# Expert stage of a mixture-of-experts layer: tiles of 256 tokens, stationary weights in the first product, biases as columns

## The chip, the core and the metric

The kernel runs on one core of one Trainium2 chip. The metric is the device time of one execution in microseconds (us). The core has five engines that run apart from each other and meet at semaphores: PE (TensorE, matrix products), DVE (VectorE), ACT (ScalarE), POOL (GpSimd) and SP (which here only issues transfers).

## The reference, cut to what matters

There are two layers in sequence. The first normalises the tokens, modulates them, and sends every token to 2 of 8 experts; the second is a transformer layer that the change leaves alone. Of the first layer the expert part is

```python
N = h_flat.shape[0]                                     # 16 * 256 = 4096 tokens, D = 256, E = 8, FF = 1024
hid = jax.nn.relu(jnp.einsum('nd,edf->nef', h_flat, exp_w1) + exp_b1)
eout = jnp.einsum('nef,efd->ned', hid, exp_w2) + exp_b2
y = jnp.einsum('ned,ne->nd', eout, combine)             # combine: two gates per token, else 0
return x + y.reshape(x.shape)
```

The kernel computes only the two experts that a token chose: 8192 pairs of token and expert.

## The kernel before

The function `condition_and_route` has three stages: conditioning, routing over 16 blocks of 256 tokens (`pipeline`), and the expert stage. `transformer` follows and reads the experts' rows back by gather.

**Expert stage.** Routing writes the token rows of each expert into a region of its own in memory (`dispatch`), and each region is cut into tiles of `P` = 128 tokens. Since the counts are known only at run time, the loop always runs over the largest number of tiles that can occur, `TILES` = (8192 - 128) / 128 + 8 = 71; a small table (`tile_tab`) gives the expert and the first row of each. All expert weights lie on chip in float32 (`w1`, `w2`).

Each product is made of three passes over operands that are split into an upper part (rounded to fp32r, `hi`) and the rest (`lo`): hi·hi, hi·lo, lo·hi (`PASSES`). So for every tile the weights of its expert are split again, 4 pieces of 128x512 for each product: ACT rounds (`upper_w1` L406, `upper_w2` L412), then DVE subtracts for the first product (`lower_w1` L714) and POOL for the second (L351).

One tile t goes this way:

- SP loads the rows (`load`) and both biases, repeated over 128 partitions (`load_b1` 512 KB, `load_b2`).
- PE turns the rows (`turn_in` L478, 2 transposes); ACT and DVE split them (`take_in` L394, `lower_tokens` L719).
- `up` (L489): 12 products, the turned tokens stationary, 512 columns of weights moving; the result has tokens on the partitions. DVE adds the bias (`take_hidden` L709).
- PE turns the 1024 hidden features (`turn_hidden` L497, 8 transposes); ACT takes the relu and rounds (`relu` L400), DVE makes the rest (`lower_hidden` L700).
- `down` (L507): 24 products of 256 columns; DVE adds the bias (`take_out` L727), SP stores.

The order on every engine is that of the code: each engine runs `tile_loop` with a `body` of its own, and an engine that waits holds everything behind it. The stage is a pipeline over two tiles: in one turn of the loop PE runs the first product of tile t and the second of tile t - 1,

```python
            if a_tile(t - 1):
                turn_hidden(t - 1)
            if a_tile(t):
                up(t)
            if a_tile(t + 1):
                turn_in(tile.ahead(1))
            if a_tile(t - 1):
                down(t - 1)
```

and DVE finishes the hidden features of tile t - 1 first, then splits `w1` for tile t + 1, two pieces before and two after the second half of `take_hidden`.

Of the kernel before, what the change touches and what calls it, by code (L numbers as in the profile page):

```python
# [7 lines left out]
F32 = mybir.dt.float32  # L8
# [8 lines left out]
P = 128  # L17
# [8 lines left out]
REGION = B * T + P  # L26
TILES = (K * B * T - P) // P + E
# [83 lines left out]
def condition_and_route(nc, ctx, io, keep):  # L111
# [78 lines left out]
    htok = [xin[0][:, i, :] for i in range(2)]  # L190
    y = xin[1][:, 0, :]
    hid = token_rows[:].rearrange("p i n -> p (i n)")
# [6 lines left out]
    b1 = [sb(f"b1_row{i}", [P, FF]) for i in range(2)]  # L199
# [17 lines left out]
    cond = cond_weights(nc, sb, ada_w, sty_w2)  # L217
# [12 lines left out]
    def _(sp):  # L230
# [1535 lines left out]
```

## Time and profile before

| | us |
|---|---|
| median of 3 runs | 1499.03 (1496.92 to 1502.69) |
| the profiled execution, its own time | 1499.17 |
| its span in the trace | 1497.0 |
| PE busy / DVE busy / ACT busy / POOL busy | 1295.6 / 1138.4 / 963.0 / 738.3 |

The span is the time from the first to the last event of the trace; some 2 us of the execution's time lie outside it. A busy PE is not a PE at its peak, since its products overlap: of two that follow each other closely, the distance between their starts is the cost, not the duration printed. "PEclk" and the column after POOL in a table of stretches are the TensorE clock that was granted, as a share of full speed (1.0 is 2.4 GHz, 0.5 is 1.2 GHz). The expert stage lies between about 165 and 689 us.

### The profile page before, as it was taken

To read this page: it belongs to the slowest core of one execution; us is meant where nothing else is said; L and a number is where in the kernel's file an instruction comes from. 1 tells how busy PE (TensorE), PEld (TensorE's weight loads), DVE (VectorE), ACT (ScalarE), POOL (GpSimd) and SP (SyncE) were. 2 spreads that over 40 slices of the span, in tenths; PEclk is the share of its full clock that TensorE was granted. 3 is DMA by queue.
4 is the path that set the end of the run, shared out by engine and by line. 5 is a ranking of instruction groups with operands and counts; after the bars stand their busy time and mean duration, and the time that the engine had idled before them with its cause. 6 is when DMAs were issued, how large, how long until landed. Compare 5 with 4: busy or idle time off the path is not lost. (4 is left out here: it accounts for less than half of the span.)

```text
span 1497.0 us, 36973 instructions
## 1 busy us (share of the span) xinstructions
PE 1295.6 (87%) x9225; PEld 1126.6 (75%) x9225; DVE 1138.4 (76%) x3159; ACT 963.0 (64%) x2326; POOL 738.3 (49%) x645
## 2 busy tenths in 40 slices
PE   2666499999999999994579999999999999999996
PEld 2555388888888888883468878888788877788875
DVE  3888799999999999995657666676666775666652
ACT  2222388888888888881166666666666666676671
POOL 1677488888888888884212323223232332322211
PEclk9999999999999999996799999999999999999997
DMA  3676333333433434344666665566655566555520
GB/s 115 210 239 221 125 133 127 126 126 126 134 127 125 128 124 135 127 127 141 202 222 191 215 190 184 168 189 211 196 182 172 185 210 204 175 184 167 184 78 14
DMA packets 197678, 241.07 MB, mean 161 GB/s; under 512 B 20720, under 2 KB 176560, under 8 KB 197616
## 3 DMA queue, kind: packets, MB, share of 16 engines
q1 hardware_dynamic: 184816, 202.70, 42.9%
q10 hardware_dynamic: 6624, 20.84, 4.3%
q0 software_dynamic: 6176, 16.79, 3.2%
q8 instruction: 28, 0.46, 0.1%
q14 instruction: 34, 0.28, 0.1%
HBM read 196.36 MB, written 39.71 MB: 158 GB/s over the span
## 5 line engine op out<-in xcount | busy, mean ns | idle before, releaser
L351 POOL TENSOR_TENSOR w_lo<-w,w_hi 128x512 fp32r<-128x512 f32 x284 | 422.7, 1518 | 100.2 <-ACT w_hi L412 100.2
L1176 ACT ACTIVATE bias<-bias,neg_max 128x256 f32<-128x256 f32 x512 | 255.3, 501 | 200.8 <-DVE neg_max L1488 200.3
L714 DVE TENSOR_TENSOR w_lo<-w,w_hi 128x512 fp32r<-128x512 f32 x284 | 302.0, 1102 | 1.0 <-ACT w_hi L406 1.0
L412 ACT ACTIVATE w_hi<-w 128x512 fp32r x284 | 179.2, 632 | 54.0 <-PE ps_y L507 35.8
L1488 DVE CUSTOM_DVE_ANT_0 bias<-ps_s,bias 128x256 f32<-128x256 f32 x512 | 194.2, 416 | 20.2 <-PE ps_s L1264 13.1
L406 ACT ACTIVATE w_hi<-w 128x512 fp32r x284 | 173.3, 632 | 21.7 <-DVE tile_tab L683 11.0
L1128 POOL TENSOR_TENSOR act_lo<-up_f,act_hi 128x512 fp32r<-128x512 f32 x64 | 82.5, 1289 | 209.3 <-ACT act_hi L1220 209.3
L507 PE MATMUL ps_y<-w_hi,hidT_hi 128*128 128x256 f32 x568 | 168.8, 297 | 14.8 <-DVE hidT_lo L700 14.2
L1262 PE MATMUL ps_s<-mask_f,minus_ident 128*128 128x256 f32 x512 | 155.4, 325 | 28.4 <-DVE neg_max L1488 15.9
L1276 PE MATMUL ps_p<-const,bias 128*128 128x128 f32 x1024 | 157.5, 277 | 13.7 <-ACT bias L1176 13.6
L507 PE MATMUL ps_y<-w_hi,hidT_lo 128*128 128x256 f32 x568 | 161.7, 285 | 0.0
L507 PE MATMUL ps_y<-w_lo,hidT_hi 128*128 128x256 f32 x568 | 161.3, 284 | 0.0
L1110 POOL TENSOR_TENSOR rstd<-mv,minus_half 128x2 f32<-128x2 f32 x32 | 23.1, 722 | 258.9 <-DVE mv L1547 171.9
L1262 PEld LDWEIGHTS ps_s<-mask_f,minus_ident 128*128 128x128 f32 x512 | 99.7, 195 | 60.9 <-DVE neg_max L1488 34.4
L1264 PE MATMUL ps_s<-k_stack,q_stack 128*128 128x256 f32 x512 | 135.2, 285 | 0.0
L1276 PEld LDWEIGHTS ps_p<-const,bias 128*128 128x128 f32 x1024 | 117.1, 141 | 22.4 <-issue 12.4
L507 PEld LDWEIGHTS ps_y<-w_hi,hidT_hi 128*128 128x128 f32 x568 | 109.2, 192 | 32.0 <-DVE hidT_lo L700 23.7
L489 PE MATMUL ps_h<-w_hi,htokT_hi 128*128 128x512 f32 x284 | 118.2, 416 | 0.9 <-DVE htokT_lo L719 0.9
L1182 ACT ACTIVATE probT<-ps_p 128x512 f32<-128x512 f32 x176 | 102.3, 581 | 24.7 <-PE ps_p L1276 24.7
L489 PE MATMUL ps_h<-w_hi,htokT_lo 128*128 128x512 f32 x284 | 112.8, 397 | 0.0
L489 PE MATMUL ps_h<-w_lo,htokT_hi 128*128 128x512 f32 x284 | 111.9, 394 | 0.0
L507 PEld LDWEIGHTS ps_y<-w_lo,hidT_hi 128*128 128x128 f32 x568 | 109.4, 193 | 0.0
(266 smaller groups left out, 3330.3 us busy)
## 6 DMA issues: line engine op xcount, KB each, us to landing
bias<-bias_dram SPq DMA_DIRECT2D x128, 512.0 KB, 3.8
b_row<-b_dram SPq DMA_DIRECT2D x71, 512.0 KB, 3.6
w<-w_dram ACTq DMA_DIRECT2D x32, 512.0 KB, 4.7
xin<-dispatch SPq DMA_DIRECT2D x71, 128.0 KB, 2.2
b_row<-b_dram SPq DMA_DIRECT2D x71, 128.0 KB, 3.1
expert_out<-xin SPq DMA_DIRECT2D x71, 128.0 KB, 1.7
q_stack<-q_hi_rows SPq DMA_DIRECT2D x64, 128.0 KB, 2.9
k_stack<-k_hi_rows SPq DMA_DIRECT2D x64, 128.0 KB, 2.9
```

The costliest lines, as they stand in the source:

```text
L351: pool.tensor_tensor(w2_part["lo"][:, k, :], w2_piece(e, k), w2_part["hi"][:, k, :].bitcast(F32), ALU.subtract).then_inc(sem("w2_split"), 1)
L406: act.activation(w1_part["hi"][:, k, :], w1_piece(e, k), ACT.Copy).then_inc(sem("w1_upper"), 1)
L412: act.activation(w2_part["hi"][:, k, :], w2_piece(e, k), ACT.Copy).then_inc(sem("w2_upper"), 1)
L489: last = pe.matmul(ps_h[i][:, :], htokT[a][:, c, :], w1_part[b][:, k, :], start=(c == 0 and n == 0), stop=(c == C - 1 and n == 2))
L507: last = pe.matmul(ps_y[:, 0:D], hidT[a][:, f * P:(f + 1) * P], w2_part[b][:, k, (f % 2) * D:(f % 2 + 1) * D], start=(f == 0 and n == 0), ...
L714: dve.tensor_tensor(w1_part["lo"][:, k, :], w1_piece(e, k), w1_part["hi"][:, k, :].bitcast(F32), ALU.subtract).then_inc(sem("w1_split"), 1)
L1176: act.activation(head_rows(h, j), head_rows(h, j), ACT.Exp, scale=-1.0, bias=neg_max[par][:, h, j:j + 1], accum_out=total[par][:, h, j:j + ...
L1182: act.activation(probT[:, h % (2 * GROUP), :, :], halves(ps_p[h % 2][:, :]), ACT.Copy).then_inc(sem("pT_scalar"), 1)
L1262: pe.matmul(ps_s[h % 2][:, j * T:(j + 1) * T], minus_ident[:], mask_f[par][:, j, :], start=True, stop=False)
L1264: last = pe.matmul(ps_s[h % 2][:, j * T:(j + 1) * T], q_stack[par][:, h, j * P:(j + 1) * P].bitcast(F32R), k_stack[par][:, h // 2, :].bitc ...
L1276: last = pe.transpose(ps_p[h % 2][:, kt * T + j * P:kt * T + (j + 1) * P], head_rows(h, j)[:, kt * P:(kt + 1) * P], ident)
L1488: dve.tensor_tensor_reduce(head_rows(h, j), ps_s[h % 2][:, j * T:(j + 1) * T], head_rows(h, j), -1.0, LARGEST, ALU.add, ALU.min, neg_max[p ...
```

## The change

The tile grows to `TOK` = 256 tokens, so `TILES` is (8192 - 256) / 256 + 8 = 39. In `up` the weights become the stationary operand and the 256 turned tokens the moving one: 48 products of 256 columns for a tile, and the result comes out with the features on the partitions, so that `turn_hidden` goes away. The bias is then one number per partition: `b1` is loaded once as columns, ACT adds it within the relu (one instruction for each of 8 feature blocks) and writes float32 to a ring of four slots, `hid`. DVE rounds pairs of blocks (`split_hidden`), and DVE (pairs 0 and 2) and POOL (pairs 1 and 3) make the rest (`lower_pair`). `down` has 48 products into two banks. The work on a tile is no longer spread over two turns of the loop: `up(t)`, `turn_in(t + 1)` and `down(t)` stand behind each other. Small weights of the conditioning move into the room of the last expert's `w1`, and ACT waits for their use before it loads that.

```diff
-REGION = B * T + P
-TILES = (K * B * T - P) // P + E
+TOK = 256
+REGION = B * T + TOK
+TILES = (K * B * T - TOK) // TOK + E
...
-
-    htokT = {n: sb(f"htokT_{n}", [P, C, P], F32R) for n in ("hi", "lo")}
-    hidT = {n: sb(f"hidT_{n}", [P, FF], F32R) for n in ("hi", "lo")}
+    htok = [buf[:] for buf in xin]
+    y = h2
+    hid = columns[:].rearrange("p i n -> p (i n)").rearrange("p (s m) -> p s m", s=HID_SLOTS)
+
+    htokT = {n: sb(f"htokT_{n}", [P, C, TOK], F32R) for n in ("hi", "lo")}
+    hidT = {n: sb(f"hidT_{n}", [P, F, TOK], F32R) for n in ("hi", "lo")}
...
-    b1 = [sb(f"b1_row{i}", [P, FF]) for i in range(2)]
+    b1 = sb("b1_columns", [P, E, F])
...
+    ps_t = bank("ps_t")
+    ps_h = [bank(f"ps_h{i}") for i in range(F // 2)]
+    ps_y = [bank(f"ps_y{j}") for j in range(J)]
+    ps_h0, ps_h1, ps_logit, ps_rank = ps_h
+    ps_back = ps_y[0]
...
+    def lower_pair(eng, t, g):
+
+        rows = slice(2 * g, 2 * g + 2)
+        slots = slice(2 * g % HID_SLOTS, 2 * g % HID_SLOTS + 2)
+        return eng.tensor_tensor(hidT["lo"][:, rows, :], hid[:, slots, :], hidT["hi"][:, rows, :].bitcast(F32), ALU.subtract)
...
+        sp.dma_start(b1[:], io["b1"]).then_inc(sem("b1_in"), 16)
...
-        def load_b1(tile):
-            wait_free(sp, sem("hid_ready"), 2 * (tile.t - 1), alone=True)
-            row = io["b1"][bass.ds(expert_of(tile.t), 1), :].rearrange("e n -> (e n)")
-            sp.dma_start(b1[tile.par][:], row.partition_broadcast(P)).then_inc(sem(f"b1_in{tile.par}"), 16)
...
+        def lower_hidden(t, g):
+            wait_alone(pool, sem("hid_rounded"), 2 * t + g // 2 + 1)
+            lower_pair(pool, t, g).then_inc(sem("hidT_odd"), 1)
+
+        def lower_w2(t, e, k):
+            wait_alone(pool, sem("w2_upper"), PARTS * t + k + 1)
+            pool.tensor_tensor(w2_part["lo"][:, k, :], w2_piece(e, k), w2_part["hi"][:, k, :].bitcast(F32),
+                               ALU.subtract).then_inc(sem("w2_split"), 1)
+
         def body(tile):
...
+            t = tile.t
+            if a_tile(t):
+                e = pool.value_load(tile_tab[0:1, 0, bass.ds(t, 1)], min_val=0, max_val=E - 1)
+                lower_hidden(t, 1)
+                lower_w2(t, e, 0)
+                lower_w2(t, e, 1)
+                lower_hidden(t, 3)
+                lower_w2(t, e, 2)
+                lower_w2(t, e, 3)
...
+            wait_free(act, sem("up_done"), F * t)
+            act.activation(htokT["hi"][:], ps_t[:, :].rearrange("p (c m) -> p c m", c=C), ACT.Copy).then_inc(sem("htokT_upper"), 1)
+
+        def relu(t, e, f):
+            if f % 2 == 0:
+                g = f // 2
+                wait_alone(act, sem("up_done"), F * t + f + 2)
+                wait_free(act, sem("hidT_odd" if g % 2 else "hidT_even"), 2 * t + g // 2, alone=True)
+            act.activation(hid[:, f % HID_SLOTS, :], ps_h[f // 2][:, (f % 2) * TOK:(f % 2 + 1) * TOK], ACT.Relu,
+                           bias=b1[:, bass.ds(e, 1), f:f + 1].rearrange("p e f -> p (e f)")).then_inc(sem("hid_ready"), 1)
+
+        def upper_w1(t, e, k):
+            wait_free(act, sem("up_done"), F * (t - 1) + 4 * (k // C + 1), alone=True)
+            act.activation(w1_part["hi"][:, k, :], w1_piece(e, k), ACT.Copy).then_inc(sem("w1_upper"), 1)
+
+        def upper_w2(t, e, k):
+            wait_free(act, sem("w2_used"), PARTS * (t - 1) + k + 1, alone=True)
+            act.activation(w2_part["hi"][:, k, :], w2_piece(e, k), ACT.Copy).then_inc(sem("w2_upper"), 1)
+
+        def expert_of(t):
+            return act.value_load(tile_tab[0:1, 0, bass.ds(t, 1)], min_val=0, max_val=E - 1)
 
         def body(tile):
             t = tile.t
-            if a_tile(t - 1):
-                relu(t - 1)
+            if a_tile(t):
+                e = expert_of(t)
+                for f in range(4):
+                    relu(t, e, f)
             if a_tile(t + 1):
-                upper_w1(t + 1)
+                ahead = expert_of(t + 1)
+                for k in range(PARTS):
+                    upper_w1(t + 1, ahead, k)
                 take_in(t + 1)
             if a_tile(t):
-                upper_w2(t)
-
+                for f, pieces in ((4, ()), (5, (0,)), (6, (1,)), (7, (2, 3))):
+                    relu(t, e, f)
+                    for k in pieces:
+                        upper_w2(t, e, k)
...
+                for j in range(J):
+                    last = pe.transpose(ps_t[:, c * TOK + j * P:c * TOK + (j + 1) * P], htok[tile.par][:, j, c * P:(c + 1) * P], ident)
             last.then_inc(sem("tile_turned"), 1)
 
         def up(t):
             pe.wait_ge(sem("htokT_split"), t + 1)
...
-
-        def turn_hidden(t):
-            pe.wait_ge(sem("hid_ready"), 2 * (t + 1))
-            wait_free(pe, sem("hidT_split"), 2 * t)
             for f in range(F):
-                last = pe.transpose(ps_th[f // 4][:, (f % 4) * P:(f % 4 + 1) * P], hid[:, f * P:(f + 1) * P], ident)
-            last.then_inc(sem("hid_turned"), 1)
+                if f % 4 == 0:
+                    pe.wait_ge(sem("w1_split"), PARTS * t + C * (f // 4 + 1))
+                if f % 2 == 0:
+                    wait_free(pe, sem("hid_ready"), F * (t - 1) + f + 2)
+                for c in range(C):
+                    for n, (a, b) in enumerate(PASSES):
+                        last = pe.matmul(ps_h[f // 2][:, (f % 2) * TOK:(f % 2 + 1) * TOK],
+                                         w1_part[a][:, C * (f // 4) + c, (f % 4) * P:(f % 4 + 1) * P], htokT[b][:, c, :],
+                                         start=(c == 0 and n == 0), stop=(c == C - 1 and n == 2))
+                last.then_inc(sem("up_done"), 1)
 
         def down(t):
-            pe.wait_ge(sem("hidT_split"), 2 * (t + 1))
             wait_free(pe, sem("y_ready"), t)
             for k in range(PARTS):
                 pe.wait_ge(sem("w2_split"), PARTS * t + k + 1)
+                pe.wait_ge(sem("hidT_odd" if k % 2 else "hidT_even"), 2 * t + k // 2 + 1)
                 for f in (2 * k, 2 * k + 1):
...
+                    for j in range(J):
+                        for n, (a, b) in enumerate(PASSES):
+                            last = pe.matmul(ps_y[j][:, 0:D], hidT[a][:, f, j * P:(j + 1) * P],
+                                             w2_part[b][:, k, (f % 2) * D:(f % 2 + 1) * D],
+                                             start=(f == 0 and n == 0), stop=(f == F - 1 and n == 2))
...
         def body(tile):
             t = tile.t
-            if a_tile(t - 1):
-                turn_hidden(t - 1)
             if a_tile(t):
                 up(t)
             if a_tile(t + 1):
...
+        def split_hidden(t, g):
+            dve.wait_ge(sem("hid_ready"), F * t + 2 * (g + 1))
+            wait_free(dve, sem("w2_used"), PARTS * (t - 1) + g + 1)
+            rows = slice(2 * g, 2 * g + 2)
+            slots = slice(2 * g % HID_SLOTS, 2 * g % HID_SLOTS + 2)
+            rounded = dve.tensor_copy(hidT["hi"][:, rows, :], hid[:, slots, :])
+            if g % 2:
+                rounded.then_inc(sem("hid_rounded"), 1)
+            else:
+                rounded.then_inc(sem("hid_upper"), 1)
+                dve.wait_ge(sem("hid_upper"), 2 * t + g // 2 + 1)
+                lower_pair(dve, t, g).then_inc(sem("hidT_even"), 1)
...
-            dve.tensor_tensor(y, ps_y[:, 0:D], b2[tile.par][:], ALU.add).then_inc(sem("y_ready"), 1)
+            wait_free(dve, sem(f"y_sent{tile.par}"), 16 * tile.before)
+            for j in range(J):
+                last = dve.tensor_tensor(y[tile.par][:, j, :], ps_y[j][:, 0:D], b2[tile.par][:], ALU.add)
+            last.then_inc(sem("y_ready"), 1)
 
         def body(tile):
             t = tile.t
             if a_tile(t + 1):
                 e = dve.value_load(tile_tab[0:1, 0, bass.ds(t + 1, 1)], min_val=0, max_val=E - 1)
-            if a_tile(t - 1):
-                lower_hidden(t - 1)
+                for k in range(PARTS):
+                    lower_w1(t + 1, e, k)
+                lower_tokens(t + 1)
             if a_tile(t):
-                take_hidden(tile, 0)
-            if a_tile(t + 1):
-                lower_w1(t + 1, e, 0)
-                lower_w1(t + 1, e, 1)
-            if a_tile(t):
-                take_hidden(tile, 1)
-            if a_tile(t + 1):
-                lower_tokens(t + 1)
-                lower_w1(t + 1, e, 2)
-                lower_w1(t + 1, e, 3)
+                for g in range(F // 2):
+                    split_hidden(t, g)
             if a_tile(t - 1):
                 take_out(tile.ahead(-1))
```

How the order on DVE changes: the rows below are what DVE runs in one turn of `tile_loop` (a straight copy of it ahead of the loop). `columns` is the room of `hid` after the change, `token_rows` that of `hid` before and of `y` after. Before:

```order
L700 SCALAR_TENSOR_TENSOR hidT_lo<-ps_th,hidT_hi 128x512 [waits hidT_upper] x2
L709 TENSOR_TENSOR token_rows<-ps_h,b_row 128x512 [waits hid_turned,b1_in1,w1_used]
L714 ISA [waits w1_upper]
L714 TENSOR_TENSOR w_lo<-w,w_hi 128x512
...
L709 TENSOR_TENSOR token_rows<-ps_h,b_row 128x512 [waits w1_used]
L719 TENSOR_TENSOR htokT_lo<-ps_t,htokT_hi 128x256 [waits htokT_upper]
...
L727 TENSOR_TENSOR xin<-ps_y,b_row 128x256 [waits b2_in0,w2_used]
```

And after, the last piece of `w1` of the next tile and all that follows it:

```order
L736 ISA [waits w1_upper]
L736 TENSOR_TENSOR w_lo<-w,w_hi 128x512
L741 TENSOR_TENSOR htokT_lo<-ps_t,htokT_hi 128x512 [waits htokT_upper]
L726 CAST hidT_hi<-columns 128x512 [waits w2_used,hid_ready]
L232 TENSOR_TENSOR hidT_lo<-columns,hidT_hi 128x512 [waits hid_upper]
L726 CAST hidT_hi<-columns 128x512 [waits w2_used,hid_ready] x2
L232 TENSOR_TENSOR hidT_lo<-columns,hidT_hi 128x512 [waits hid_upper]
L726 CAST hidT_hi<-columns 128x512 [waits w2_used,hid_ready]
L750 TENSOR_TENSOR token_rows<-ps_y,b_row 128x256 [waits b2_in0,w2_used]
L750 TENSOR_TENSOR token_rows<-ps_y,b_row 128x256
```

The hidden features of a tile stood first in the turn and belonged to the tile before; now they belong to the tile of this turn and stand behind all the split weights and tokens of the next.

On PE, in one turn of the loop before (the 12 products of `up`, of which the last stand here, then the turned tokens of the next tile, then `down` of the tile before):

```order
L489 MATMUL ps_h<-w_hi,htokT_lo 128x512
L478 MATMUL ps_t<-const,xin 128x128 [waits htokT_split,tile_in0]
L478 MATMUL ps_t<-const,xin 128x128
L507 MATMUL ps_y<-w_hi,hidT_hi 128x256 [waits w2_split,hidT_split]
L507 MATMUL ps_y<-w_lo,hidT_hi 128x256
```

After, at the same place, where `down` is that of the tile whose `up` has just ended:

```order
L519 MATMUL ps_h<-htokT_hi,w_lo 128x256
L507 MATMUL ps_t<-const,xin 128x128 [waits htokT_split,tile_in1]
L507 MATMUL ps_t<-const,xin 128x128 x3
L527 REGISTER_ALU [waits y_ready]
L528 ISA [waits w2_split]
L532 MATMUL ps_y<-w_hi,hidT_hi 128x256 [waits hidT_even]
L532 MATMUL ps_y<-w_lo,hidT_hi 128x256
```

`y_ready` is what `take_out` of the tile before signals; it is the last thing in DVE's turn.

## Rows read from the trace of the kernel before

**Rows 1.** The page: busy time, and the 40 slices of DVE, tenths busy.

```profile
PE 1295.6 (87%) x9225; PEld 1126.6 (75%) x9225; DVE 1138.4 (76%) x3159; ACT 963.0 (64%) x2326; POOL 738.3 (49%) x645
...
DVE  3888799999999999995657666676666775666652
```

**Rows 2.** Busy time by stretch: length, PE, PEld, DVE, ACT, POOL, clock, DMA.

```profile
400.00:500.00 100.00, 97.47 (x642) 86.33 (x641) 100.00 (x141) 87.10 (x154) 83.31 (x56) 1.00 0.40 128
```

**Rows 3.** Order of time on DVE, 398 to 413 us: start, duration.

```profile
397.46 1.27 DVE L700 SCALAR_TENSOR_TENSOR hidT_lo<-ps_th,hidT_hi 128x512 fp32r<-128x512 f32 x2
...
399.25 1.52 DVE L714 TENSOR_TENSOR w_lo<-w,w_hi 128x512 fp32r<-128x512 f32 x2
...
401.62 2.75 DVE L714 TENSOR_TENSOR w_lo<-w,w_hi 128x512 fp32r<-128x512 f32 x2
404.29 0.41 DVE L727 TENSOR_TENSOR xin<-ps_y,b_row 128x256 f32<-128x256 f32 x1
404.63 1.27 DVE L700 SCALAR_TENSOR_TENSOR hidT_lo<-ps_th,hidT_hi 128x512 fp32r<-128x512 f32 x2
```

**Rows 4.** Order of time on all engines, 400 to 415 us.

```profile
405.95 0.39 PE L507 MATMUL ps_y<-w_hi,hidT_hi 128*128 128x256 f32 x1 [0.17 <-DVE hidT_lo L700]
...
406.29 0.37 ACT L394 ACTIVATE htokT_hi<-ps_t 128x256 fp32r<-128x256 f32 x1
...
407.12 2.79 ACT L412 ACTIVATE w_hi<-w 128x512 fp32r x4 [0.46 <-PE ps_y L507]
...
407.98 5.96 POOL L351 TENSOR_TENSOR w_lo<-w,w_hi 128x512 fp32r<-128x512 f32 x4 [1.21 <-ACT w_hi L412]
...
408.81 0.29 PE L507 MATMUL ps_y<-w_hi,hidT_lo 128*128 128x256 f32 x1
...
410.01 1.09 ACT L400 ACTIVATE hidT_hi<-ps_th 128x512 fp32r<-128x512 f32 x2
...
410.98 2.58 ACT L406 ACTIVATE w_hi<-w 128x512 fp32r x4
```

**Rows 5.** Instructions by line: duration in ns least/median/most, first and last start.

```profile
L351 POOL TENSOR_TENSOR w_lo<-w,w_hi x284: 1263/1402/1762, 178.7 to 684.0; 128x512 fp32r<-128x512 f32 x142
L714 DVE TENSOR_TENSOR w_lo<-w,w_hi x284: 676/921/1785, 167.6 to 675.0; 128x512 fp32r<-128x512 f32 x142
L507 PE MATMUL ps_y<-w_hi,hidT_lo x568: 274/283/415, 182.4 to 688.7; 128*128 128x256 f32 x190
L1197 ACT ACTIVATE q_hi<-ps_q,q_b x32: 466/470/477, 713.4 to 1382.1; 128x256 fp32r<-128x256 f32 x32
L1553 DVE TENSOR_SCALAR h_rows<-x,mv,rstd x32: 401/1019/1376, 796.3 to 1474.9; 128x256 f32<-128x256 f32 x32
L1579 DVE TENSOR_SCALAR wq<-wq x1: 421/421/421, 707.1 to 707.1; 128x512 f32<-128x512 f32 x1
```

**Rows 6.** Order of time on PE, start of the stage, 140 to 182 us.

```profile
170.48 0.69 PE L478 MATMUL ps_t<-const,xin 128*128 128x128 f32 x2 [15.47 <-DMA xin<-dispatch]
172.10 0.80 PE L489 MATMUL ps_h<-w_hi,htokT_hi 128*128 128x512 f32 x1 [0.93 <-DVE htokT_lo L719]
```

**Rows 7.** Order of time on PE, the last tile's `down`, 682 to 692 us.

```profile
684.35 0.39 PE L507 MATMUL ps_y<-w_hi,hidT_hi 128*128 128x256 f32 x1 [2.01 <-DVE hidT_lo L700]
...
684.87 0.41 PE L507 MATMUL ps_y<-w_hi,hidT_hi 128*128 128x256 f32 x1
...
685.08 0.42 PE L507 MATMUL ps_y<-w_lo,hidT_hi 128*128 128x256 f32 x1
...
688.07 0.32 PE L507 MATMUL ps_y<-w_hi,hidT_hi 128*128 128x256 f32 x1
```

**Rows 8.** Busy time by stretch, columns as in rows 2, with the granted clock.

```profile
684.00:688.00 4.00, 3.65 (x18) 3.65 (x19) 0.30 (x1) 0.00 (x0) 1.23 (x2) 0.59 0.00 0
...
708.00:712.00 4.00, 2.80 (x8) 2.06 (x7) 0.00 (x0) 1.02 (x2) 1.65 (x5) 0.50 1.05 385
```

**Rows 9.** Order of time on DVE, the tables, 160 to 195 us.

```profile
160.74 0.74 DVE L675 TENSOR_TENSOR b_row<-tile_e,const 1x568 f32<-1x568 f32 x1
```

More of the change, by code:

```diff
@@ L285, in body @@
                 load(tile.ahead(2))
-                load_b1(tile.ahead(2))
             if a_tile(tile.t - 1):
-                store(tile.t - 1)
+                store(tile.ahead(-1))
             if a_tile(tile.t + 1):
@@ L292, in _ @@
         load(Tile(0, 0))
-        load_b1(Tile(0, 0))
         tile_loop(sp, body)
-        sp.wait_ge(sem("y_sent"), 16 * TILES)
+        for par in range(2):
+            sp.wait_ge(sem(f"y_sent{par}"), 16 * ((TILES + 1 - par) // 2))
     @block.gpsimd
@@ L367, in step @@
             b = 2 * i + par
+            if isinstance(i, int) and b == 3:
+                act.wait_ge(sem("cond_product"), 6)
             if rows:
@@ L392, in take_in @@
             act.wait_ge(sem("tile_turned"), t + 1)
-            wait_free(act, sem("w1_used"), PARTS * t)
-            act.activation(htokT["hi"][:], ps_t[:, 0:C * P].rearrange("p (c m) -> p c m", c=C), ACT.Copy).then_inc(sem("htokT_upper"), 1)
-        def relu(t):
-            act.wait_ge(sem("hid_turned"), t + 1)
-            wait_free(act, sem("w2_used"), PARTS * t)
-            for i in range(2):
-                act.activation(hidT["hi"][:, i * 512:(i + 1) * 512], ps_th[i][:, :], ACT.Relu).then_inc(sem("hidT_upper"), 1)
@@ L504, in down @@
                 pe.wait_ge(sem("w2_split"), PARTS * t + k + 1)
+                pe.wait_ge(sem("hidT_odd" if k % 2 else "hidT_even"), 2 * t + k // 2 + 1)
                 for f in (2 * k, 2 * k + 1):
-                    for n, (a, b) in enumerate(PASSES):
-                        last = pe.matmul(ps_y[:, 0:D], hidT[a][:, f * P:(f + 1) * P], w2_part[b][:, k, (f % 2) * D:(f % 2 + 1) * D],
-                                         start=(f == 0 and n == 0), stop=(f == F - 1 and n == 2))
+                    for j in range(J):
[3 more added lines that the diff above has]
+                                             start=(f == 0 and n == 0), stop=(f == F - 1 and n == 2))
                 last.then_inc(sem("w2_used"), 1)
@@ L694, in _ @@
         dve.wait_ge(sem("tables_ready"), 1)
-        def lower_hidden(t):
-            for i in range(2):
-                dve.wait_ge(sem("hidT_upper"), 2 * t + i + 1)
-                cols = slice(i * 512, (i + 1) * 512)
-                dve.scalar_tensor_tensor(hidT["lo"][:, cols], ps_th[i][:, :], 0.0, hidT["hi"][:, cols].bitcast(F32),
-                                         ALU.max, ALU.subtract).then_inc(sem("hidT_split"), 1)
-        def take_hidden(tile, i):
-            t = tile.t
-            dve.wait_ge(sem("w1_used"), PARTS * t + C * (i + 1))
-            if i == 0:
-                dve.wait_ge(sem(f"b1_in{tile.par}"), 16 * (tile.before + 1))
-                wait_free(dve, sem("hid_turned"), t)
-            dve.tensor_tensor(hid[:, i * 512:(i + 1) * 512], ps_h[i][:, :], b1[tile.par][:, i * 512:(i + 1) * 512],
-                              ALU.add).then_inc(sem("hid_ready"), 1)
+        def split_hidden(t, g):
[10 more added lines that the diff above has]
+                lower_pair(dve, t, g).then_inc(sem("hidT_even"), 1)
         def lower_w1(t, e, k):
@@ L755 @@
 UNROLL = 4
+HID_SLOTS = 4
 class Tile:
@@ L799, in pipeline, with cond_weights, place @@
     step(B // 2, 1, False, False, True)
[L802 removed]
+def cond_weights(nc, sb, room):
+    def place(rows, start, width):
+        return room[0:rows, start:start + width]
     return {
         "ids": sb("ids", [B, 1], U32), "emb": sb("emb", [B, SE]), "embT": sb("embT", [SE, B]),
[L805 to L807 removed]
+        "ada_w": place(P, 0, 2 * C * D).rearrange("p (c n) -> p c n", c=C), "sty_w2": place(SH // 2, 1024, 2 * D),
+        "hyp_w1": place(SE, 1536, SH), "hyp_w2": place(SH, 1664, SH), "sty_w1": place(SH, 1792, SH // 2),
         "a1": sb("a1", [SH, B]), "a2": sb("a2", [SH, B]), "a3": sb("a3", [SH // 2, B]),
```

90 lines of the change are left out of this document (28 added, 62 removed).

## The prediction

> **What bounds the kernel now.** I first read the page's slices: between the routing and the transformer layer lies a stretch in which DVE stands at 9 in every slice [rows 1]. The table of stretches makes this exact: in 100 us of the expert stage DVE is busy for all 100, PE for 97.5, ACT 87.1, POOL 83.3, and the clock is 1.00 [rows 2]. So the stage is bound by DVE. Then the order of time on DVE gives the price of a tile: the same instruction opens a tile at 397.46 and at 404.63, so a tile of 128 tokens takes 7.17 us [rows 3], and 71 of them 509 us. From the first product of the stage at 172.10 [rows 6] to the end of the last at 688.7 + 0.28 [rows 5] it is 517 us. PE is close behind: `down` has 24 products of 256 columns from 405.95 to 408.81, 0.12 us apart [rows 4].
>
> If only the busiest engine counted, the change would be a good one: half as many tiles, each with the same 8 pieces of weights to split. What decides, however, is that before the change no engine waits for a chain, because the hidden features that DVE treats belong to the tile before. So I follow the chain after the change through one tile.
>
> **The change part by part.**
>
> Work of PE. `up` becomes 48 products and `down` 48, each with 128x128 stationary and 256 moving, as those of `down` now: 48 x 0.12 = 5.76 us each [rows 4]. The four transposes, some 0.5 us, lie beside the chain below. PE alone would need 12.0 us a tile, 39 tiles 468 us.
>
> The chain. Let 0 be the end of `up(t)`. `down(t)` is next on PE, and it needs three things: the split hidden features, the split `w2`, and `y_ready` of tile t - 1, which DVE signals at the end of its turn. All of it stands behind the preparation of tile t + 1, half of which can't start before 0, since pieces 2 and 3 of `w1` are read until `up(t)` ends.
>
> 1. ACT rounds pieces 2 and 3: four take 2.58, the first 0.63, so 0.65 each [rows 4]: 1.3. Then the turned tokens, 128x512 out of PSUM, like the pair of relus in 1.09, 0.6 [rows 4]: 1.9.
> 2. DVE subtracts the two pieces beside it, then the tokens: 0.64, as the pair in 1.27 [rows 3]. With a handoff: 2.6.
> 3. DVE rounds pair 0. The trace has no copy of that shape, but a single-input one of 128x512 takes 0.42 [rows 5]: 3.05. The rest of pair 0, two inputs, least duration 0.68 [rows 5]: 3.8. Pair 1 rounded: 4.2.
> 4. Only now is the ring free for ACT's relus of blocks 4 and 5. With a bias per partition 256 columns take 0.47 [rows 5]; two end at 4.6.
> 5. POOL starts the rest of pair 1 at 4.2 + 0.23 (that is how long it waited behind the first piece of ACT, which began at 407.12 and took 0.63, before 407.98 [rows 4]): 4.4. It takes 1.27 at least [rows 5]: 5.7. That frees the ring for blocks 6 and 7. ACT: relu 6, a piece of `w2` (0.63), relu 7: 7.3.
> 6. DVE rounds pair 3. By now POOL is in its next piece. Beside POOL, DVE's instructions on SBUF grow: two pieces of `w1` take 1.52 where POOL has ended and 2.75 where it is at work [rows 3, 4], and a single-input one of 0.40 has a median of 1.02 [rows 5]. Ends: nothing more, or 0.6 more. I take the latter, as its row is of the same kind: 8.3.
> 7. `take_out` of the tile before, two of 0.41 [rows 3], 0.75 with their overlap: 9.05. PE has then stood still for 8.5 us.
> 8. `down` needs 5.76, and its start is slow. After an idle time of 15.5 us the first product of the stage, at 172.10, takes 0.80 [rows 6], and in the last tile, after a gap of 2.0, products are 0.21 apart from 684.87 until 688.07, with a granted clock of 0.59 over that window, the lower level of 1.2 GHz for most of it [rows 7, 8]. So some 3.2 to 4 us of each `down` go at 0.21 for 0.12, which costs 0.43 per us: 1.4 to 1.7. I take 1.6: end at 16.4. POOL does not set this: it has six instructions in a tile now for four, from 4.4 at 1.27 to 1.49 each (four took 5.96 [rows 4]), to 13.3 at most, and behind its last piece a quarter of `down`, 1.4, remains: 14.7.
> 9. `up(t + 1)` follows at once, everything for it is long ready: 5.76, full clock. Next end of `up`: 22.2.
>
> A tile of 256 tokens costs 22.2 us, where two of 128 cost 14.3. From the first product to the last it is 39 x 22.2 less about 3 for the last tile, which prepares none behind it: 863 us, against 517. That is +346.
>
> On step 6 there is a rule to weigh. By the row, DVE's single-input work grows by 0.6 beside POOL. The Trainium skill (SBUF — State Buffer, "SBUF: two separate sides") says that the port pair that the two share is locked for a whole instruction and the other blocks fully. By that rule the two pieces of `w1` in rows 3 would have taken about 3.1, not 2.75, so the trace agrees in direction and less in size; step 6 would come to 0.4 more at the worst.
>
> What costs nothing or little. SP still loads a tile two turns ahead, now over 20 us, and stores behind `take_out`, where nothing waits for it. The 71 loads of `b1` of 512 KB go: no engine waited for one in rows 2, where DVE is never idle, so nothing. Tables for 39 tiles: five steps of 0.74 for 568 elements [rows 9] become some 0.3 shorter: -1.5. Clearing 256 rows instead of 128 and loading 256 KB for the first tile lie in the 15.5 us before the first tile [rows 6]: 0 to +2; I take 0.5. The wait of ACT for the conditioning is met long before its place in block 3 of routing: 0.
>
> Sum against the profiled execution: 1499.2 + 346 - 1 = 1844. It lies within 0.2 us of the median, so no correction. A difference of under 0.5% (7.5 us) is about what a measurement of this kernel can't tell from none.
>
> **The rivals.**
>
> A, the same chain with its cheap ends: relus of 0.37, as ACT takes for 256 columns without a bias [rows 4], no loss of DVE beside POOL, and the clock stays at 2.4 GHz. Then y_ready is at 8.0 and the tile takes 8.0 + 5.8 + 5.8, or by POOL's last piece (12.8 + 1.4 + 5.8) 20.0: 780 - 3 - 517 = +260, 1758. For it: half the terms are upper ends of what rows show. Against it: the clock fell behind a gap of only 2.0 us [rows 7].
>
> B, the clock comes back late. With PE at 2.80 busy of 4 the clock stayed at 0.50 for a whole window [rows 8]. If all of `down` ran at 0.21, it would take 10.1 for 7.4, a tile 24.9: +451, 1949; half of that if it holds in every second tile, 1897.
>
> C, not slower: the engines overlap after all, as the sums of work suggest. The mechanism would be that `down(t)` does not wait for `y_ready` and the hidden features behind tile t + 1's preparation. A tile then takes as long as the busiest engine: PE, 12.0 and some 0.5 of small gaps, 39 of them 488, less 517 = -29, 1469. It decides at 517 / 39 = 13.2 us a tile: the stall of PE between `up` and `down` would have to be under 1.2 us instead of 8.5. Against it stand the order of DVE and PE and the fact that step 1 alone takes 1.9.
>
> D, POOL becomes the bound through contention. If its six instructions took the 1.76 that is the most seen [rows 5], the last piece would end at 4.4 + 10.6 = 15.0, and `down` at 16.6: the same as step 8. Beyond that it would add to the sum; with 2.0 each, 23.7 a tile, 1901.
>
> **How the numbers follow.** The chain as worked out 0.62; A 0.17; B 0.08; D 0.08; C 0.03; other than these, 0.02. The time is that of the chain, 1844. The range takes in A with a little below it, B in every second tile and most of D, and leaves out C and the far end of B: 1745 to 1915. Faster by over 0.5%: 0.03; within 0.5%: 0.01; slower: 0.96.
>
> **What would show it.** Right, if in the profile after: 39 tiles between 172 and about 1035 us, the same instruction on DVE 22 us apart; PE idle for 8 to 9 us ahead of the first product of `down`, released by DVE's `take_out` or POOL; PE's share near 55% in the stage, DVE's and ACT's under 60%; a granted clock under 1.00 and products of `down` 0.21 apart at first. Step 1 is wrong if ACT's pieces 2 and 3 start before `up` ends; step 8 if the clock stays at 1.00; step 6 if DVE's third and fourth rounding take 0.43. The whole is wrong if a tile takes under 20 or over 24 us. I am least sure of the clock and of POOL beside DVE.

## The result, and the profile after

Over four runs the changed kernel took 1511.71 us (median; 1508.70 to 1515.01), the kernel before beside it 1497.97. The ratio is 1.0086, with a 95% interval of 1.0050 to 1.0123: slower by just under 1%. The prediction said 1844 us, between 1745 and 1915. Only its sign was right, and by luck, as told below; the size was wrong by 332 us.

The page of the profiled execution, to be laid beside [rows 1]:

```profile
span 1507.0 us, 35099 instructions
...
PE 1286.2 (85%) x9859; PEld 1157.2 (77%) x9859; DVE 993.0 (66%) x2956; ACT 834.4 (55%) x2208; POOL 636.0 (42%) x595
...
PE   2666499999999999993589999999899999999996
...
DVE  3887567667766766775557666666666765667552
```

In the expert stage DVE stood at 9 in every slice and now stands at 5 to 7; PE still stands at 9. The table of stretches says the same of the 100 us shown in [rows 2] (length, PE, PEld, DVE, ACT, POOL, clock, DMA share, GB/s):

```profile
400.00:500.00 100.00, 94.67 (x762) 91.42 (x761) 69.90 (x99) 60.75 (x129) 62.30 (x46) 1.00 0.17 52
```

PE is 95% busy where the prediction had put it near 55%, and the granted clock is 1.00, as in each of the stretches from 200 to 600 us. PE does not stand still for 8.5 us in a tile. The order of time on PE, 400 to 430 us (start, duration, and in brackets the idle time before and what ended it), shows the two gaps that it has:

```profile
401.13 0.60 PE L507 MATMUL ps_t<-const,xin 128*128 128x128 f32 x4
402.21 0.38 PE L532 MATMUL ps_y<-w_hi,hidT_hi 128*128 128x256 f32 x1 [0.48 <-DVE token_rows L750]
...
408.46 0.38 PE L519 MATMUL ps_h<-htokT_hi,w_hi 128*128 128x256 f32 x1 [0.24 <-DVE htokT_lo L741]
```

The order of time on DVE over one tile of 256 tokens, where [rows 3] have two of 128:

```profile
407.53 0.68 DVE L741 TENSOR_TENSOR htokT_lo<-ps_t,htokT_hi 128x512 fp32r<-128x512 f32 x1
408.13 0.41 DVE L726 CAST hidT_hi<-columns 128x512 fp32r<-128x512 f32 x1
408.57 0.69 DVE L232 TENSOR_TENSOR hidT_lo<-columns,hidT_hi 128x512 fp32r<-128x512 f32 x1
409.18 0.42 DVE L726 CAST hidT_hi<-columns 128x512 fp32r<-128x512 f32 x1
410.33 1.00 DVE L726 CAST hidT_hi<-columns 128x512 fp32r<-128x512 f32 x1 [0.73 <-ACT columns L420]
411.37 1.67 DVE L232 TENSOR_TENSOR hidT_lo<-columns,hidT_hi 128x512 fp32r<-128x512 f32 x1
412.95 1.52 DVE L726 CAST hidT_hi<-columns 128x512 fp32r<-128x512 f32 x1
414.40 0.74 DVE L750 TENSOR_TENSOR token_rows<-ps_y,b_row 128x256 f32<-128x256 f32 x2
418.23 2.51 DVE L736 TENSOR_TENSOR w_lo<-w,w_hi 128x512 fp32r<-128x512 f32 x4 [3.09 <-ACT w_hi L425]
420.66 0.68 DVE L741 TENSOR_TENSOR htokT_lo<-ps_t,htokT_hi 128x512 fp32r<-128x512 f32 x1
```

`htokT_lo` opens a tile at 407.53 and at 420.66: 13.1 us a tile (13.15 over many), not 22.2. Two tiles of 128 took 14.37 (7.18 each in the mean). For the same rows the stage has become 8% faster. But there are 39 tiles of 256, so 9984 rows, where 71 of 128 were 9088: 39 x 13.15 = 513 us, against 71 x 7.18 = 510. The gain by row has gone into 10% more rows. All of these are rows without a pair, since the pairs are 8192 in both kernels.

**What is late.** DVE waits some 3 us in each tile for ACT (`w_hi`), and ACT and POOL wait too, while PE, which should be the bound at 12 us, waits 0.7. These rows of ACT and POOL, in order of time, close a loop through all of them:

```profile
402.95 0.84 ACT L420 ACTIVATE columns<-ps_h,b_columns 128x256 f32<-128x256 f32 x2 [1.73 <-POOL hidT_lo L232]
404.13 2.20 ACT L425 ACTIVATE w_hi<-w 128x512 fp32r x4 [0.33 <-issue]
...
409.46 0.84 ACT L420 ACTIVATE columns<-ps_h,b_columns 128x256 f32<-128x256 f32 x2 [2.66 <-DVE hidT_lo L232]
...
416.10 0.84 ACT L420 ACTIVATE columns<-ps_h,b_columns 128x256 f32<-128x256 f32 x2 [1.72 <-POOL hidT_lo L232]
```

```profile
409.75 1.30 POOL L232 TENSOR_TENSOR hidT_lo<-columns,hidT_hi 128x512 fp32r<-128x512 f32 x1 [4.50 <-DVE hidT_hi L726]
411.05 3.14 POOL L357 TENSOR_TENSOR w_lo<-w,w_hi 128x512 fp32r<-128x512 f32 x2
414.63 1.27 POOL L232 TENSOR_TENSOR hidT_lo<-columns,hidT_hi 128x512 fp32r<-128x512 f32 x1 [0.43 <-DVE hidT_hi L726]
```

Read it backwards from 416.10. ACT's relus of blocks 2 and 3 write to ring slots 2 and 3, which POOL must have read for pair 3 of the tile before (414.63 to 415.9). POOL needs DVE's rounding of pair 3 (412.95), which stands behind the rest of pair 2 (411.37) and its rounding (410.33), which need ACT's relus 4 and 5 (409.46). These wait for slots 0 and 1, read by DVE at 408.57, behind tokens and weights that wait for ACT's `w_hi` of 404.13, which stands behind ACT's relus at 402.95: the same instruction as at 416.10, one tile and 13.15 us earlier. The ring of four slots passes a tile's eight blocks in two rounds, and no engine has slack along it. In it, DVE pays for POOL: a rounding takes 0.42 while POOL rests and 1.00 and 1.52 beside it, a subtraction 0.69 and 1.67.

The waits of the whole stage, 200 to 660 us (us in total, times, longest), show which engines lose:

```profile
POOL hidT_lo L232 <- DVE hidT_hi L726: 176.8, 71, 4.5
DVE w_lo L736 <- ACT w_hi L425: 104.8, 35, 3.1
ACT columns L420 <- DVE hidT_lo L232: 92.2, 35, 2.8
ACT columns L420 <- POOL hidT_lo L232: 75.1, 69, 1.7
...
PE ps_y L532 <- DVE token_rows L750: 16.2, 34, 0.5
...
PE ps_h L519 <- DVE htokT_lo L741: 6.5, 31, 0.2
```

**The account of the 10 us between the spans.** From the stage's first transposes to the end of its last product it was 170.48 to 689.0, 518.5 us [rows 5, 6]; it is now 171.07 to 695.1, 524.0. Of this +5.5 the steady tiles are +3, the rest the ends. The steady tiles don't have the waits of 2.41 and 3.72 us that stand ahead of the second `up` and the last `down`. From the order of time on PE, the first tile and these two:

```profile
171.07 1.11 PE L507 MATMUL ps_t<-const,xin 128*128 128x128 f32 x4 [17.37 <-DMA xin<-dispatch]
...
184.90 0.39 PE L519 MATMUL ps_h<-htokT_hi,w_hi 128*128 128x256 f32 x1 [2.41 <-DVE htokT_lo L741]
...
687.55 0.44 PE L532 MATMUL ps_y<-w_hi,hidT_hi 128*128 128x256 f32 x1 [3.72 <-DVE token_rows L750]
```

The transformer stage starts 6.8 us later (698.4 for 691.6), and its unchanged code took 808.6 us for 805.4.

### The profile page after: what moved, and what is told of

Read it like the earlier page. It is cut to its first block and busy times, and to the rows that moved or that the text cites. A ratio compares the mean times of both kernels' runs of the same rounds, so it can differ in the third digit from the quotient of the medians.

```text
span 1507.0 us, 35099 instructions
## 1 busy us (share of the span) xinstructions
PE 1286.2 (85%) x9859; PEld 1157.2 (77%) x9859; DVE 993.0 (66%) x2956; ACT 834.4 (55%) x2208; POOL 636.0 (42%) x595
## 5 line engine op out<-in xcount | busy, mean ns | idle before, releaser
L420 ACT ACTIVATE columns<-ps_h,b_columns 128x256 f32<-128x256 f32 x312 | 134.6, 471 | 190.1 <-DVE hidT_lo L232 102.8
L357 POOL TENSOR_TENSOR w_lo<-w,w_hi 128x512 fp32r<-128x512 f32 x156 | 222.0, 1436 | 0.3
L519 PE MATMUL ps_h<-htokT_hi,w_hi 128*128 128x256 f32 x624 | 182.5, 293 | 11.0 <-DVE htokT_lo L741 10.4
L232 POOL TENSOR_TENSOR hidT_lo<-columns,hidT_hi 128x512 fp32r<-128x512 f32 x78 | 100.1, 1283 | 209.2 <-DVE hidT_hi L726 209.2
L736 DVE TENSOR_TENSOR w_lo<-w,w_hi 128x512 fp32r<-128x512 f32 x156 | 102.7, 715 | 119.7 <-ACT w_hi L425 119.7
L519 PE MATMUL ps_h<-htokT_hi,w_lo 128*128 128x256 f32 x624 | 178.5, 286 | 0.0
L519 PE MATMUL ps_h<-htokT_lo,w_hi 128*128 128x256 f32 x624 | 178.3, 286 | 0.0
L532 PE MATMUL ps_y<-w_lo,hidT_hi 128*128 128x256 f32 x624 | 177.3, 284 | 0.0
L726 DVE CAST hidT_hi<-columns 128x512 fp32r<-128x512 f32 x156 | 128.8, 825 | 31.6 <-ACT columns L420 29.7
L519 PEld LDWEIGHTS ps_h<-htokT_hi,w_hi 128*128 128x128 f32 x624 | 121.4, 195 | 18.8 <-issue 12.6
```

The costliest lines, as they stand in the source:

```text
L232: return eng.tensor_tensor(hidT["lo"][:, rows, :], hid[:, slots, :], hidT["hi"][:, rows, :].bitcast(F32), ALU.subtract)
L357: pool.tensor_tensor(w2_part["lo"][:, k, :], w2_piece(e, k), w2_part["hi"][:, k, :].bitcast(F32), ALU.subtract).then_inc(sem("w2_split"), 1)
L420: act.activation(hid[:, f % HID_SLOTS, :], ps_h[f // 2][:, (f % 2) * TOK:(f % 2 + 1) * TOK], ACT.Relu, bias=b1[:, bass.ds(e, 1), f:f + 1]. ...
L519: last = pe.matmul(ps_h[f // 2][:, (f % 2) * TOK:(f % 2 + 1) * TOK], w1_part[a][:, C * (f // 4) + c, (f % 4) * P:(f % 4 + 1) * P], htokT[b ...
L532: last = pe.matmul(ps_y[j][:, 0:D], hidT[a][:, f, j * P:(j + 1) * P], w2_part[b][:, k, (f % 2) * D:(f % 2 + 1) * D], start=(f == 0 and n = ...
L726: rounded = dve.tensor_copy(hidT["hi"][:, rows, :], hid[:, slots, :])
```

## The experiments

The theories. **L**: the loop just read sets 13.15. **P**: PE is the bound and its small waits of 0.48 and 0.24 add to its work; take them away and the tile shrinks by as much. Beside these, two statements to test: that the change is a gain by the row, which the rounding up to tiles of 256 takes back; and that the sum of 22.2 us priced another program, one in which `down` of the same tile is next on PE.

**The same kernel again**, beside the others of its group.

> The changed kernel once more, as the base for the three beside it. Expected as measured: 1.009 of the kernel before, 1509 to 1512 us, 13.1 us a tile.

It took 1517.23 us against 1506.43, a ratio of 1.0066 [1.0046, 1.0087]. Groups of runs differ by some us, and so kernels of different groups are compared by their ratios.

**`take_early`: DVE takes `down`'s result out before pair 2.** The wait ahead of `down` is then gone.

```diff
             if a_tile(t):
-                for g in range(F // 2):
+                for g in range(2):
                     split_hidden(t, g)
             if a_tile(t - 1):
                 take_out(tile.ahead(-1))
+            if a_tile(t):
+                for g in range(2, F // 2):
+                    split_hidden(t, g)
```

> Changed kernel with one move on DVE: take_out of the tile before stands between the second and the third pair of hidden features, in a gap in which DVE is idle for 0.7 us a tile, instead of behind the fourth. That takes PE's wait for y_ready (0.49 us a tile) away. Theory L (a loop ACT, DVE, POOL through the four-slot room of the hidden features sets the period of 13.13 us, and PE's two waits are only its slack): no change, within 3 us of the changed kernel, PE's idle time moves to the wait for the turned tokens. Theory P (PE is the bound, each of its waits adds itself): 39 x 0.49 = 19 us faster, about 1492 us.

1514.74 us, ratio 1.0053 [1.0034, 1.0071]: not measurably other than the changed kernel. PE's wait moved to the start of `up`, where it is 0.96 to 1.02 us; the two together were 0.72. From the order of time on PE:

```profile
409.58 0.38 PE L519 MATMUL ps_h<-htokT_hi,w_hi 128*128 128x256 f32 x1 [1.02 <-DVE htokT_lo L741]
...
422.74 0.38 PE L519 MATMUL ps_h<-htokT_hi,w_hi 128*128 128x256 f32 x1 [0.96 <-DVE htokT_lo L741]
```

P falls. A wait of the busiest engine that something slower sets can't be removed where it shows.

**`own_room`: pair 3 gets a room of its own**, in `xn`, which is idle in this stage, so that ACT's relus 2 and 3 needn't wait for POOL's last piece of hidden features. `own_room_take_early` does both edits.

```diff
-    hid = columns[:].rearrange("p i n -> p (i n)").rearrange("p (s m) -> p s m", s=HID_SLOTS)
+    hid_room = [columns[:, 0, :], columns[:, 1, :], columns[:, 0, :], keep["xn"][:].rearrange("p j d -> p (j d)")]
+    hid = [room.rearrange("p (s m) -> p s m", s=2) for room in hid_room]
...
-                wait_free(act, sem("hidT_odd" if g % 2 else "hidT_even"), 2 * t + g // 2, alone=True)
+                wait_free(act, sem("hidT_odd" if g % 2 else "hidT_even"), 2 * t + g // 2 - g % 2, alone=True)
```

> Changed kernel with a room of its own for pair 3 of the hidden features (in xn, unused in this stage), so that pairs 1 and 3, which POOL finishes, no longer share one and ACT's relus of blocks 2 and 3 of the next tile need not wait for POOL. Theory L: the loop gets about 3 us shorter and PE becomes the bound at 12.4 us a tile: 39 x 0.73 = 28 us faster, about 1483 us. Theory P: nothing changes on PE's waits for DVE's last instruction and for the tokens: 1510 us.

1506.70 us, ratio 1.0000 [0.9978, 1.0022], so 0.7% under the changed kernel: the loop was touched, but for a third of the 28 us that I expected. Most tiles take 12.86 and every fourth 13.16, 12.92 in the mean, for 13.15: 9 us over 39 tiles. The other half of the ring, slots 0 and 1 for pairs 0 and 2, took over the waiting:

```profile
ACT columns L420 <- DVE hidT_lo L232: 154.4, 35, 5.0
```

> Both edits. Theory L: as own_room alone, 1483 us, PE without waits in the stage. Theory P: as take_early alone, 1492 us.

1509.50 us, ratio 1.0015 [0.9998, 1.0031]: no better than `own_room` alone. Both theories had expected more, 1483 and 1492 us.

**`down_same_turn`: the program that I had priced.** The one edit on PE:

```diff
-            if a_tile(t - 1):
-                down(t - 1)
+            if a_tile(t):
+                down(t)
```

> The changed kernel with the order on PE that the prediction worked with: up(t), turn_in(t + 1), down(t) instead of down(t - 1). If the chain of the prediction was sized rightly and only the order was misread: 22.2 us a tile, about 1844 us (1745 to 1915), PE idle some 8 us a tile and the clock falling in each. If the sum itself was wrong as well, the time lies outside that range; if the order of down does not matter: 1510 us.

1917.84 us, ratio 1.2737 [1.2690, 1.2784]. PE's order of time, and below it the stretches of a tile with the granted clock:

```profile
416.54 0.60 PE L507 MATMUL ps_t<-const,xin 128*128 128x128 f32 x4
426.70 0.58 PE L532 MATMUL ps_y<-w_hi,hidT_hi 128*128 128x256 f32 x1 [9.55 <-DVE token_rows L750]
```

```profile
403.00:407.00 4.00, 4.00 (x19) 4.00 (x20) 0.00 (x0) 0.00 (x0) 2.78 (x3) 0.50 0.31 101
407.00:411.00 4.00, 4.00 (x32) 4.00 (x32) 0.00 (x0) 0.00 (x0) 0.00 (x0) 0.92 0.21 62
...
417.00:426.00 9.00, 0.14 (x2) 0.00 (x0) 7.53 (x11) 5.28 (x11) 4.33 (x4) 0.74 0.00 0
```

The turned tokens stand at 416.54 and next at 440.44: 23.9 us a tile. The chain of the sum is that of this program: the stall ahead of `down` exists in this program, with the releaser and the cold first 4 us of `down` that the prediction named, and one line's order is worth 400 us. The price was low by 1.7 a tile, and 1917.84 lies 3 us above the range of 1745 to 1915. By the words of the expectation the sum was then wrong as well, though by much less than the order was; where, is told below.

**`tiles36` and `before78`: the rows.** `tiles36` is the changed kernel without its last three tiles (9216 rows; it leaves out what tokens would lie in those three). `before78` is the kernel before with 78 tiles, the seven more being padding (9984 rows); its numbers for the tiles are laid out a little wider for it.

```diff
-TILES = (K * B * T - TOK) // TOK + E
+TILES = (K * B * T - TOK) // TOK + E - 3
```

```diff
-TILES = (K * B * T - P) // P + E
+TILES = (K * B * T - P) // P + E + 7
```

> The changed kernel with 36 tiles for 39 (9216 rows, near the 9088 of the kernel before, instead of 9984); it leaves out the last three tiles. If the period of a tile is all that counts: 3 x 13.13 = 39 us faster than the changed kernel, about 1471 us. If a part of the loss lies elsewhere (start, end, the transformer), the difference to the kernel before, 1498, is smaller than 35.5 tiles of 13.13 against 71 of 7.17 would give (-43 us).

> The kernel before with 78 tiles for 71, that is 9984 rows as the changed kernel has. Expected 7 x 7.17 = 50 us slower than the kernel before, about 1548 us; so for equal rows the change would be 37 us faster, and the coarser tile takes it back. Rival: the seven tiles without work cost less, then rounding up is not what the change loses.

`tiles36` took 1479.47 us, ratio 0.9826 [0.9796, 0.9855]; `before78` 1559.65, ratio 1.0346 [1.0314, 1.0378]. The rounding up takes the gain back; this holds from both sides. `tiles36` is 26 us under the kernel before in its group, where 36 tiles of 13.15 against 71 of 7.18 would be 36. In the profiles the stage itself, from its first transposes to its last product, is 33 us shorter (485.6 for 518.5). So 3 us are lost at the ends of the stage, and where the other 7 go no run shows. With equal rows the changed kernel would be at about 1.0066 / 1.0346 = 0.973 of the kernel before: 2.7% faster. Seven more tiles of 128 cost 3.5%.

**`four_rooms`: a room for each pair.** The ring is gone; pair 2 goes to the room of `zeros`, made wider, pair 3 to `xn`.

```diff
-    hid = columns[:].rearrange("p i n -> p (i n)").rearrange("p (s m) -> p s m", s=HID_SLOTS)
+    hid_room = [columns[:, 0, :], columns[:, 1, :], zeros_room[:], keep["xn"][:].rearrange("p j d -> p (j d)")]
+    hid = [room.rearrange("p (s m) -> p s m", s=2) for room in hid_room]
...
-                wait_free(act, sem("hidT_odd" if g % 2 else "hidT_even"), 2 * t + g // 2, alone=True)
+                wait_free(act, sem("hidT_odd" if g % 2 else "hidT_even"), 2 * t + g // 2 - 1, alone=True)
```

> A room of its own for each of the four pairs of hidden features (the fourth in xn, the third in the room of the zeros, made 1 KB wider), so that no relu of ACT waits for a pair of the same tile. With pair 3 alone moved, a tile took 12.86 us (13.13 at each turn of the unrolled loop) for 13.15, and DVE still stood 0.73 us a tile waiting for relus 4 and 5. Theory L2 (the room was one edge of the loop, what is left is DVE's own row of instructions with that wait in it, slowed by POOL): the 0.73 goes, a tile takes PE's 12.4 us or a little more, 39 x 0.4 = 16 us faster than own_room, ratio to the kernel before about 0.99. Rival: DVE's work beside POOL grows by what the wait gave, since it then collides more; ratio as own_room, 1.00.

1482.17 us, ratio 0.9868 [0.9846, 0.9890]: faster than both kernels. A tile takes 12.30, and the same 100 us read:

```profile
400.00:500.00 100.00, 100.00 (x816) 98.06 (x815) 99.45 (x106) 68.44 (x140) 78.46 (x50) 1.00 0.18 55
```

DVE has gone from 70 to 99 with 7% more tiles in the stretch. It has lost its waits, and the pieces of `w1` that ran while POOL rested now run beside it. Its order of time:

```profile
408.89 1.51 DVE L726 CAST hidT_hi<-xn 128x512 fp32r<-128x512 f32 x1
410.33 0.74 DVE L750 TENSOR_TENSOR token_rows<-ps_y,b_row 128x256 f32<-128x256 f32 x2
410.99 6.24 DVE L736 TENSOR_TENSOR w_lo<-w,w_hi 128x512 fp32r<-128x512 f32 x4
417.15 0.68 DVE L741 TENSOR_TENSOR htokT_lo<-ps_t,htokT_hi 128x512 fp32r<-128x512 f32 x1
```

Four pieces of `w1` take 6.24 where they took 2.51. In the changed kernel DVE stood still for 30% of a tile of 13.15, some 4 us; 0.85 of that has become speed, and the rest comes back as longer instructions beside POOL. DVE is the bound again, at 12.3. PE shows no idle time, but the third and fourth quarter of `down` start 0.04 to 0.12 late behind POOL's `w_lo`, and this with the slower start behind each is the 0.36 beyond PE's own 11.94.

> The same, with take_out between pairs 1 and 2. Theory L2: PE's wait for y_ready (0.48 us a tile) goes and no gap is lost on DVE for it: equal to four_rooms or up to 5 us faster. Rival: since take_out stands ahead of pair 3, POOL and the next split of w1 come 0.7 us later, slower by up to 10 us, as it was with one room (1.0015 against 1.000).

1494.49 us, ratio 0.9924 [0.9896, 0.9951], with 12.6 a tile: slower than `four_rooms`. DVE is again 99% busy from 400 to 500 us, so taking out early delays what stands behind it; PE is now idle for 0.2 us a tile before POOL's `w_lo` ends, where `four_rooms` has no idle time on PE.

**`pool_light`: the changed kernel without most of POOL's work.** From the second tile on POOL subtracts 2 of the 512 columns of each piece of `w2`, so the lower parts of `w2` are left out. Order, waits and rooms stay.

```diff
-            pool.tensor_tensor(w2_part["lo"][:, k, :], w2_piece(e, k), w2_part["hi"][:, k, :].bitcast(F32),
+            n = 512 if isinstance(t, int) and t == 0 else 2
+            pool.tensor_tensor(w2_part["lo"][:, k, 0:n], w2_piece(e, k)[:, 0:n], w2_part["hi"][:, k, 0:n].bitcast(F32),
```

> The changed kernel, where POOL subtracts only 2 of 512 columns of each piece of w2 from the second tile on; it leaves out the lower parts of w2. DVE's rounding of pairs 2 and 3 and its subtraction for pair 2 take 1.0, 1.52 and 1.67 us beside POOL where they take 0.42, 0.42 and 0.69 elsewhere. If that collision is what makes the loop 13.15 us long: 2 to 2.6 us leave the loop, PE becomes the bound at 12.4 to 12.6 us, 25 us faster than the changed kernel, ratio about 0.99. Rival (the four-slot room alone does it, whatever the length of DVE's work): under 8 us faster.

1466.26 us, ratio 0.9750 [0.9728, 0.9773]. A tile takes 11.94, PE's own work with no gap. DVE's order of time, at the places of 411.37 and 412.95 of the changed kernel, with 0.69 for 1.67 and 0.43 for 1.52:

```profile
411.38 0.92 DVE L727 CAST hidT_hi<-columns 128x512 fp32r<-128x512 f32 x1 [0.81 <-ACT columns L421]
412.33 0.69 DVE L232 TENSOR_TENSOR hidT_lo<-columns,hidT_hi 128x512 fp32r<-128x512 f32 x1
413.70 0.43 DVE L727 CAST hidT_hi<-columns 128x512 fp32r<-128x512 f32 x1 [0.68 <-ACT columns L421]
```

The gain over the changed kernel is about 50 us where I expected half, since I had put PE alone at 12.4. The ring is still there, but without DVE's losses beside POOL its loop is shorter than PE's work. The edit takes away POOL's own time too. That time did not lie in the loop: in the changed kernel POOL's two pieces of `w2` end at 414.19, and POOL then waits 0.43 for DVE's rounding of pair 3. The gain also shows what PE's two waits stand for. Their idle time is 0.72 us a tile, but 13.15 - 11.94 is 1.21, since at each break the products lose their overlap as well (0.52 and then 0.22 apart around 408.46, for 0.12). So neither the ring nor the contention makes 13.15 alone: without the ring, or without most of the contention, a tile takes 12.3 or less.

## Why the prediction was wrong, by its own steps

**The step that failed** is the first sentence under "The chain": "`down(t)` is next on PE". It is not. PE's turn reads

```python
            if a_tile(t):
                up(t)
            if a_tile(t + 1):
                turn_in(tile.ahead(1))
            if a_tile(t - 1):
                down(t - 1)
```

and the diff leaves its last two lines alone; it only takes `turn_hidden` away. The section on the change says that "the work on a tile is no longer spread over two turns of the loop" and, ahead of the last piece of PE's order, that "`down` is that of the tile whose `up` has just ended". Both are wrong. Rows of the order name buffers, not tiles, and look alike for `down(t)` and `down(t - 1)`; I filled in the tile from the wrong one. With `down(t - 1)`, everything that `down` needs belongs to DVE's and POOL's turn before, and the chain runs beside `up` and `down`, not between them. Steps 1 to 9 priced a stall of 8.5 us that this program doesn't have: its waits in a tile of 13.15 are 0.48 and 0.24.

That "slower" came out right is luck. It was forecast from the stall; it came from the loop through the ring, from 10% more rows, and from the ends of the stage.

**The steps in the program for which they were written**, by `down_same_turn`, with the end of `up` at 416.54. Step 1: ACT's start after the gate, expected at once, came 0.35 later (its third piece at 416.89); the turned tokens were ready at 2.0 for 1.9. Steps 2 to 4: 5.2 for 4.6 at the end of relu 5, by handoffs of 0.1 to 0.4 that I had left out. Step 6 was the largest miss. I let one DVE instruction grow by 0.6 beside POOL; three did:

```profile
421.84 0.88 DVE L726 CAST hidT_hi<-columns 128x512 fp32r<-128x512 f32 x1 [0.82 <-ACT columns L420]
422.76 1.64 DVE L232 TENSOR_TENSOR hidT_lo<-columns,hidT_hi 128x512 fp32r<-128x512 f32 x1
424.31 1.49 DVE L726 CAST hidT_hi<-columns 128x512 fp32r<-128x512 f32 x1
```

Pair 3 was rounded at 9.3 for 8.3, and step 7 ended at 9.9 for 9.05. `down` and `up` took 13.7 from 426.70 to 440.44, for 13.1 in steps 8 and 9: the products stood 0.21 apart until 431.55, so for 4.9 us where step 8 had 3.2 to 4 (the clock was at 0.50, 1.2 GHz, in the first 4 us of the tile before and at 0.92 in the next window). Together 23.9 for 22.2.

**The terms that were right.** A product of 256 columns 0.12 apart, whichever operand is stationary: 11.94 us a tile by `pool_light`, for 12.0. A relu with a bias per partition 0.47; DVE's copy of 128x512 0.42 by itself. The loads of `b1`: the DMA share fell from 0.40 to 0.17 in the 100 us and no wait shows it. The tables took 1.3 us less, for 1.5. The first tile still started no earlier: its load of 256 KB was issued when the one of 128 KB had been, at 168.41 for 168.54, and PE waited 17.37 us for it where 15.5 stood [rows 6].

**The rivals.** C, "not slower", came nearest, with a chance of 0.03: its mechanism (`down` doesn't wait behind the next tile's preparation) is what the code does. Its number, 1469, was too low by its gaps: I gave PE 0.5 a tile beyond 12.0, the loop made it 1.15, which is 25 us over 39 tiles, and the start and end of the stage are some 9 more. The place at which it turns is 517 / 39 = 13.26 us a tile (the text has 13.2). The measured 13.15 lies just under it, so the tiles alone decide nothing, and the ends of the stage make it slower. A, B and D priced the same wrong chain (in D, 15.0 and a quarter of `down` are 16.4, not 16.6, which changes nothing). D's mechanism, POOL beside DVE, is real, but acts through DVE's instructions, not through POOL's own length.

**The rule weighed at step 6.** In the changed kernel the rounding that starts at 412.95 ends at 414.47; POOL's two pieces from 411.05 end at 414.19. The rounding of 410.33 ends at 411.33; POOL's instruction at 411.05. So each of these two ends 0.28 after POOL's does, and grows with what POOL had left. The Trainium skill (SBUF — State Buffer, "SBUF: two separate sides") says that whoever holds the shared ports keeps them for the whole instruction, and these rows agree with it better than the pair of rows 3 did. The better price for the third and fourth rounding would have been POOL's remaining time plus 0.28.

**What stays open.** The transformer stage is the same code in all runs. It took 805.4 us in the profile of the kernel before and 808.6 in that of the changed one, but 819 in the one of `before78`. So 3 of the 10 us between the two spans lie there, and profiles of unchanged code differ by more than that; no experiment here separates them from chance.

## What to carry to other kernels

Before a chain is priced on an engine, write the tile's number beside every instruction of the loop's turn, for the awaited and for the waiting engine; names of buffers don't show which turn of a software pipeline is meant. When a larger tile rounds up more rows, compare time by row and count of rows apart: here 8% was won by the row and 10% more rows ran. When engines that are all under 75% busy still hold up the busiest, follow one instruction back to itself a tile earlier; the buffer that closes that loop is what to enlarge, and contention is what will then take back part of it.

## What the runs showed of the hardware

POOL and DVE on 128x512 of float32 in SBUF: DVE's rounding took 0.42 by itself and up to 1.52 beside POOL, its two-input subtraction 0.69 and 1.67; POOL's own piece 1.27 and 1.57 to 1.75. Removing most of POOL's work made the kernel 3% faster though POOL was busy for only 62% of the stage. In `down_same_turn`, TensorE's clock was at 0.50 for 4 us in the two tiles read, each behind an idle time of some 9.5 us (9.55 for the one shown), with products 0.21 apart; behind the changed kernel's waits of 0.48 it stayed at 1.00 from 200 to 600 us.
